# Graph convolution and GRU layer on one core: first group's setup without large GpSimd work, in another order

## The chip, the core and the metric

The kernel runs on one core of one Trainium2 chip. The metric is device time in microseconds. A program has five engines with a queue each: TensorE (PE), VectorE (DVE), ScalarE (ACT), GpSimd (POOL) and SyncE (SP), which here only issues DMAs.

## The reference, cut to what matters

Input `x` is 32 graphs x 256 nodes x 128 features in float32, `adj` is a 0/1 matrix of 256 x 256 for each graph.

```python
xc = transpose(x)                                  # features x nodes
h = relu(bn1(conv1(xc)))                           # 1x1 convolution
h = bn2(conv2(h))                                  # 17 taps along the nodes, padding 8
x_conv = transpose(relu(h + xc))
s = x @ w_se.T + b_se                              # 3 numbers a node
A = exp(-squared_distance(s)) * mask
x_nmp = A @ relu(x @ w_msg.T + b_msg)
gi, gh = concat(x_conv, x_nmp) @ w_ih.T + b_ih, x @ w_hh.T + b_hh
r, z = sigmoid(gi_r + gh_r), sigmoid(gi_z + gh_z)
out = layernorm(x + (1 - z) * tanh(gi_n + r * gh_n) + z * x)
```

## The kernel before, in words

The 32 graphs are taken in four groups of 8 (`NG`, `GB`), 2048 nodes each, in chunks of 512 columns. A float32 product is made of three matmuls in the rounded type fp32r: each operand is split into a high part, written by ACT (a copy into the fp32r tile), and a low part, the difference, written by DVE. `three` issues hi x hi, lo x hi and hi x lo (L324 is its matmul).

conv2 has 17 taps. The nodes of a graph lie in four phases (node number mod 4), and the kernel uses nine products (`PRODUCTS`, n = 0 to 8) in place of 16 phase pairs. Each has a "slot" of the activations (H3, D2, D3, E1, F0, F1, E3, F2, F3: a phase of conv1's output `H`, or differences of phases) and a weight set, 4 or 5 tap positions each: single taps of one phase f, or sums of taps. Product 0 uses the sum over all four phases (S0123), products 1 and 2 the sums 0+2 and 1+3, product 3 the sum 0+1, product 6 the sum 2+3, and products 4, 5, 7 and 8 the taps of phases 0, 1, 2 and 3. The results lie in `conv2_bank` in turn; ACT `shared` copies products 0, 3 and 6 out, DVE `product` adds the other six to these copies (`prod_used`), DVE `conv_sum` puts phases together and adds `x`, ACT `relu2` and DVE `conv_lo` make c_hi and c_lo.

Program order, for group 0 alone, is: conv1 on 4 chunks, "messages" for graphs 0 to 5 (relu(x W_msg), and the 3 numbers s), then `mix_stage(0, True)`: nine products of conv2, with other work put between them by `first_between`: messages 6 and 7, the transposes of the distance factors (`turn_rows`, read out by ACT `operands`), the distance matmuls (`distances`), and the gathers of the messages with A (`gather`). ACT `weights` is the exp, DVE `mask` the product with adj, ACT `sums_hi` and DVE `sums_lo` split the gathered sums into m_hi and m_lo. Then comes `gru_stage(0)`: per chunk, gate matmuls on x, m and c; in the same stage run conv1 and the messages of group 1. A loop runs `gru_stage(g)`, `mix_stage(g + 1, False)` for the other groups.

Setup that only group 0 pays: the tap sums (five tiles of 128 x 512), their hi and lo parts (`sum_hi`, `setup_sum_lo`), the hi and lo parts of the taps (`taps_hi` at L771, one ACT instruction of 2048 columns; `setup_taps_lo` at L947, four of 512), those of the gate weights (`gates_hi`, L775 and L777; `setup_gates_lo`, L926 and L927), and the slots of E and F over a whole group at once (`slot_high` L646, `slot_low` L989, `slot_f` L985). Before, POOL makes the tap sums 0+2 and 1+3 (L853), E low (L856, 1088 columns) and E high (L859, 1088 columns); DVE makes the sums 0+1, 2+3 (L922) and all four (L1309).

What sets the order is the program order of each engine's queue and semaphores: an instruction that waits holds all that stand behind it on its engine. SP's queue is the same: the issue of a DMA waits for a count, and later issues wait behind it. Buffers are shared in group 0: `x` holds four tap sums and later the real x, `ef` holds E and F, `adj[:, 1]` holds the rest of the gate weights, and `hn` and `z` hold small pieces.

```python
            def product(g, j, side, first):
                dve.wait_ge(s_ready, 3 * g + j + 1)
                dve.wait_ge(conv2_done, NP * g + n + 1)
```

Of the kernel before, what the change touches and what calls it, by code (L numbers as in the profile page):

```python
# [17 lines left out]
ALU = mybir.AluOpType  # L18
# [4 lines left out]
P = 128  # L23
# [53 lines left out]
def build(nc, xt_d, xn_d, adj_d, first_d, wsm_d, wcv_d, idn_d, bmsg_d, out_d):  # L77
    with ExitStack() as ctx:
# [53 lines left out]
        S_first = [x[:, CH:2 * CH], ef[:, SL:SL + CH], ef[:, 0:CH]]  # L132
# [4 lines left out]
        w_hhr = hn[:, 1, 0:P]  # L137
        w_rest = adj[:, 1, :, :, :].rearrange("p b m n -> p (b m n)")[:, 0:(NW - NF) * P]
# [4 lines left out]
        bmsg = z[0:2, 1, P:P + MW]  # L143

# [37 lines left out]
        bn1_ready, pool_sums_ready, idn_loaded = sem("bn1_ready"), sem("pool_sums_ready"), sem("idn_loaded")  # L182
# [3 lines left out]
        sum23_ready = sem("sum23_ready")  # L186
# [42 lines left out]
        def _(sp):  # L229
# [47 lines left out]
            sp.dma_start(w_rest, wsm_d[:, P:]).then_inc(gatesw_loaded, 16)  # L277
            sp.wait_ge(gatesw_ready, 1)
            load_adj(0, 1)
            load_adj_late(0, 2)  # L280
            sp.wait_ge(sum23_ready, 1)
            for k in range(NC):
                load_x(0, k)
            load_adj_late(0, 3)
            sp.wait_ge(cw_ready, NP - 1)
            for k in range(NC):
                load_xn(0, k)
            for s in range(2):
                sp.wait_ge(msg_done, 2 * s + 6)
                load_xs(1, s)  # L290
# [31 lines left out]
        def _(pe):  # L322
# [70 lines left out]
            def conv2(g, n, first):  # L393
# [9 lines left out]
                if first and n == 6:  # L403
                    pe.wait_ge(sum23_ready, 1)
                elif first:
                    pe.wait_ge(cw_ready, n + 1 if n < 6 else n)
# [17 lines left out]
            def first_between(n):  # L424
# [7 lines left out]
                elif n == 2:  # L432
                    distances(0, 0)
                    turn_rows(0, 1, True)
                elif n == 3:
# [151 lines left out]
        def _(act):  # L587
# [65 lines left out]
            def shared(g, j, first):  # L653
# [4 lines left out]
                if first:  # L658
                    act.wait_ge(*((cw_ready, 2), (slot_diff, 3), (slot_lo, 6))[j])
# [8 lines left out]
            def mix_stage(g, first):  # L668
                if first:
                    message(0, 6)  # L670
                    message(0, 7)
                    shared(g, 0, first)
                    slot_high(E1, E_all[:, 1], elow_ready, 1)
                    sum_hi(0)
                    operands(0, 0, True)
                    slot_high(F0, F_one, slot_diff, 1)
                    sum_hi(3)
                    gates_hi()
                    weights(g, 0)
# [5 lines left out]
                    slot_high(F1, F_one, slot_diff, 2)  # L685
                else:
# [8 lines left out]
                sums_hi(g, 0)  # L695
                shared(g, 1, first)
                weights(g, 4)
                if first:
                    slot_high(E3, E_all[:, 3], ehigh_ready, 1)
                    slot_high(F2, F_one, slot_diff, 3)  # L700
                sums_hi(g, 1)
                weights(g, 5)
                if first:
                    slot_high(F3, F_one, slot_diff, 4)
# [4 lines left out]
                weights(g, 7)  # L709
                sums_hi(g, 2)  # L710
# [72 lines left out]
            for k in (1, 2, 3):  # L783
                relu1(0, k, True)
            for k in (1, 2, 3):
                h3_hi(0, k)
            act.wait_ge(taps_loaded, 32)
            nc.scalar.activation(cw_hi[:, TAPS - 1:TAPS, :], last_tap, ACT.Copy).then_inc(cwhi_ready, 1)
            message(0, 0)
            act.wait_ge(tapsum_ready, 1)  # L790
            sum_hi(4)
            message(0, 1)
            d_hi(0, 0)
            message(0, 2)
# [18 lines left out]
        def _(pool):  # L813
# [41 lines left out]
            pool.wait_ge(h_ready, NC)  # L855
            nc.gpsimd.tensor_tensor(E_all[:, 0:2], H[:, 0:2, :], H[:, 2:4, :], ALU.subtract).then_inc(elow_ready, 1)  # L856
            pool.wait_ge(va_ready, NC)
            flat = H[:, :, :].rearrange("p a b -> p (a b)")
            nc.gpsimd.tensor_tensor(E_all[:, 2:4], H[:, 2:4, :],  # L859
                                    flat[:, 1:2 * SL + 1].rearrange("p (a b) -> p a b", a=2),  # L860
                                    ALU.subtract).then_inc(ehigh_ready, 1)
# [13 lines left out]
        def _(dve):  # L875
# [504 lines left out]
```

## Time and profile before

| what | us |
|---|---|
| median of 3 runs | 320.26 |
| the 3 runs | 319.72, 320.26, 322.0 |
| the profiled execution | 320.76 |
| its span, first to last instruction | 318.6 |
| TensorE busy in the span | 300.3 (94%) |
| VectorE busy | 251.5 (79%) |
| ScalarE busy | 155.9 (49%) |
| GpSimd busy | 31.1 (10%) |

The profiled execution is 2.16 us longer than its span; this part lies around the program. Times of rows count from the span's start. Mean granted TensorE clock: 0.982 of full speed.

### The profile page before, as it was taken

The page shows a single profiled execution, that of the slowest core. Times are in us where ns is not written, and L with a number is a line of the kernel's source. Part 1 is how long each engine was busy: PE and PEld are TensorE (multiplying, and loading weights), DVE is VectorE, ACT ScalarE, POOL GpSimd, SP SyncE. Part 2 cuts the span into 40 slices and gives each one's busy share as a digit, 9 for nine tenths or more (in the row PEclk, how much of TensorE's full clock was granted, in tenths as well). Part 3 has the DMA queues.
Part 4 walks back from the last instruction along what each step waited for, and adds up shares of the span by engine and source line. Part 5 has one row for each costly group of instructions (what it writes and reads, how often), then busy time and mean ns, then how long its engine had stood idle before and what let it go on. Part 6 is the DMA issues. An engine that isn't in the chain of part 4 may idle for free.

```text
span 318.6 us, 4624 instructions
## 1 busy us (share of the span) xinstructions
PE 300.3 (94%) x1422; PEld 240.6 (76%) x1422; DVE 251.5 (79%) x666; ACT 155.9 (49%) x326; POOL 31.1 (10%) x53
## 2 busy tenths in 40 slices
PE   8669989899999999999999999999999999999990
PEld 6457767778888778888888778888888778888860
DVE  3995869867977996967987996966987996963794
ACT  3753834338775622237775622237776613324345
POOL 3631000000000051000000041000000032000113
PEclk9959999999999999999999999999999999999997
DMA  7500161171210321171210231181210031150002
GB/s 224 214 1 2 65 224 41 66 265 64 69 34 32 103 97 68 69 263 37 80 47 21 88 122 66 66 263 35 66 51 14 32 132 66 44 154 0 0 35 99
DMA packets 12257, 27.23 MB, mean 85 GB/s; under 512 B 1363, under 2 KB 2133, under 8 KB 12117
## 3 DMA queue, kind: packets, MB, share of 16 engines
q1 hardware_dynamic: 12244, 27.08, 25.1%
q8 instruction: 6, 0.10, 0.1%
q14 instruction: 7, 0.05, 0.1%
HBM read 22.88 MB, written 4.19 MB: 85 GB/s over the span
## 4 chain that ended last, share of the span: by engine, by line
PE 81%; DVE 11%; ACT 2%; issue 2%; DMA 2%; POOL 0%; POOLq 0%; SPq 0%; ACTq 0%; DVEq 0%
PE bank L324 78%; DMA xr<-xt_dram 2%; PE bank L516 2%; PE bank L358 1%; DVE V_lo L969 1%; DVE H L1062 1%; DVE first L1096 1%; DVE V_lo L989 1%; DVE hn L1309 1%; DVE xr L1280 0%; DVE xr L1285 0%; ACT hn L745 0%; DVE x_lo L953 0%; DVE first L1102 0%; DVE H L1077 0%
## 5 line engine op out<-in xcount | busy, mean ns | idle before, releaser
L324 PE MATMUL bank<-V_hi,cw_hi 128*128 128x512 f32 x160 | 70.5, 440 | 2.8 <-ACT EF L661 1.4
L324 PE MATMUL bank<-V_lo,cw_hi 128*128 128x512 f32 x160 | 64.9, 406 | 0.0
L324 PE MATMUL bank<-V_hi,cw_lo 128*128 128x512 f32 x160 | 64.6, 404 | 0.0
L324 PE MATMUL bank<-x_hi,w_hl 128*128 128x512 f32 x128 | 47.3, 410 | 1.1 <-DVE x_lo L953 1.1
L324 PEld LDWEIGHTS bank<-V_hi,cw_hi 128*128 128x128 f32 x160 | 30.6, 191 | 11.0 <-issue 2.5
L324 PEld LDWEIGHTS bank<-V_hi,cw_lo 128*128 128x128 f32 x160 | 30.4, 190 | 8.4
L324 PEld LDWEIGHTS bank<-V_lo,cw_hi 128*128 128x128 f32 x160 | 30.5, 190 | 7.1
L324 PE MATMUL bank<-m_hi,w_hl 128*128 128x512 f32 x96 | 35.3, 400 | 0.6 <-DVE m_lo L1047 0.6
L324 PE MATMUL bank<-c_hi,w_hl 128*128 128x512 f32 x96 | 34.9, 396 | 0.0
L631 ACT ACTIVATE m_hi<-bank 128x512 fp32r<-128x512 f32 x16 | 9.6, 599 | 42.4 <-PE bank L324 42.4
L818 POOL TENSOR_TENSOR rstd<-first,pconst 128x4 f32<-128x4 f32 x16 | 3.5, 220 | 269.4 <-DVE first L1102 269.4
L324 PEld LDWEIGHTS bank<-x_hi,w_hl 128*128 128x128 f32 x128 | 24.1, 188 | 7.2 <-DVE x_lo L953 1.5
L1265 DVE SCALAR_TENSOR_TENSOR hn<-xr,hn 128x512 f32<-128x512 f32 x15 | 10.4, 692 | 20.5 <-ACT hn L733 20.5
L324 PE MATMUL bank<-x_lo,w_hl 128*128 128x512 f32 x64 | 25.2, 393 | 0.0
L732 ACT ACTIVATE xr<-bank,vec 128x512 f32<-128x512 f32 x16 | 11.0, 690 | 24.0 <-PE bank L324 24.0
L324 PEld LDWEIGHTS bank<-m_hi,w_hl 128*128 128x128 f32 x96 | 18.0, 188 | 5.1 <-DVE m_lo L1047 1.0
L324 PEld LDWEIGHTS bank<-c_hi,w_hl 128*128 128x128 f32 x96 | 18.0, 188 | 4.4
L324 PE MATMUL bank<-first,xr 128*128 128x132 f32 x128 | 20.0, 285 | 0.0
L666 ACT ACTIVATE c_hi<-H 128x512 fp32r<-128x512 f32 x16 | 10.2, 639 | 19.1 <-DVE H L1077 15.5
L1062 DVE SCALAR_TENSOR_TENSOR H<-bank,vec,EF 128x512 f32<-128x512 f32 x16 | 11.9, 746 | 9.1 <-PE bank L324 9.1
L324 PE MATMUL bank<-m_lo,w_hl 128*128 128x512 f32 x48 | 19.0, 396 | 0.0
L324 PE MATMUL bank<-c_lo,w_hl 128*128 128x512 f32 x48 | 19.0, 395 | 0.0
(135 smaller groups left out, 599.0 us busy)
## 6 DMA issues: line engine op xcount, KB each, us to landing
adj<-adj_dram SPq DMA_DIRECT2D x16, 512.0 KB, 4.4
x<-xt_dram SPq DMA_DIRECT2D x16, 256.0 KB, 3.1
xn<-xn_dram SPq DMA_DIRECT2D x16, 256.0 KB, 4.5
out_dram<-xn SPq DMA_DIRECT2D x15, 256.0 KB, 2.1
xr<-xt_dram SPq DMA_DIRECT2D x13, 256.0 KB, 3.5
xn<-wcv_dram SPq DMA_DIRECT2D x1, 1024.0 KB, 7.3
xr<-xt_dram SPq DMA_DIRECT2D x1, 768.0 KB, 6.0
adj<-wsm_dram SPq DMA_DIRECT2D x1, 512.0 KB, 7.8
```

Of the source, the lines that this page charges most:

```text
L324: return nc.tensor.matmul(out, lhs, rhs, start=start, stop=stop, skip_group_check=True)
L358: last = nc.tensor.transpose(out[:, i * N + mb * P:i * N + (mb + 1) * P], f32(U[:, i, mb]).rearrange("p b k -> p (b k)"), idn[:, :])
L516: turned = nc.tensor.transpose(turn_bank[k][:, j * P:(j + 1) * P], r[:, k % 2, j * P:(j + 1) * P], idn[:, :])
L631: nc.scalar.activation(chunk(m_hi, pair), nmp_bank[pair % 2][:, :], ACT.Copy).then_inc(mhi_ready, 1)
L666: nc.scalar.activation(phase(c_hi, c), inner(c), ACT.Relu).then_inc(chi_ready, 1)
L732: nc.scalar.activation(r[:, k % 2, :], r_bank[:, :], ACT.Tanh, bias=v(BR), scale=0.5).then_inc(r_ready, 1)
L818: nc.gpsimd.tensor_tensor(dst, src, eps.broadcast_to(shape), ALU.add).then_inc(eps_added, 1)
L969: TT(part(V_lo, H3, k), part(H, 3, k), f32(part(V_hi, H3, k)), ALU.subtract).then_inc(h3_ready, 1)
L989: TT(V_lo[:, slot, :], src, f32(V_hi[:, slot, :]), ALU.subtract).then_inc(slot_lo, 1)
L1062: STT(dst, grid(src), v(NSC2 if side else SC2), grid(shr), ALU.mult, ALU.add).then_inc(prod_used, 1)
L1096: last = nc.vector.bn_stats(stats[:, NB * k + j, :], node_rows(k)[:, j, :])
L1265: STT(hk, rk, 1.0, hk, ALU.add, ALU.mult).then_inc(gated_ready, 1)
```

## The change

POOL keeps only its small vectors. The tap sums 0+2 and 1+3, E low and E high go to DVE. The sum of all taps gets its hi and lo first, and the last tap follows. The taps are split phase by phase, each phase hi (`tap_hi`, 512 columns of stride) then lo, each counted in `cw_ready`. The first block of gate weights (`w_hhr`) moves to `z`, its split stays early; the rest of the gate weights (`w_rest`, 512 KB) is loaded into `ef` after the last F slot is made, and split at the end of the stage. `adj(0, 1)` is loaded at the start. `S_first` of products 3 and 6 moves to `xr`. PE's second `turn_rows` moves from product 2 to product 3. ACT's `operands(0, 0)` moves ahead of the split of E1. Waits change with that: x is loaded into `x` after the seventh weight set, xs for group 1 after `prod_used` 4 and 6.

```diff
-        S_first = [x[:, CH:2 * CH], ef[:, SL:SL + CH], ef[:, 0:CH]]
+        S_first = [x[:, CH:2 * CH], xr[:, 0], xr[:, 1]]
-        w_hhr = hn[:, 1, 0:P]
-        w_rest = adj[:, 1, :, :, :].rearrange("p b m n -> p (b m n)")[:, 0:(NW - NF) * P]
+        w_rest = ef[:, 0:(NW - NF) * P]
+        w_hhr = z[:, 1, CH - P:CH]
...
 SP:
             load_adj(0, 0)
-            sp.dma_start(w_rest, wsm_d[:, P:]).then_inc(gatesw_loaded, 16)
-            sp.wait_ge(gatesw_ready, 1)
             load_adj(0, 1)
             load_adj_late(0, 2)
-            sp.wait_ge(sum23_ready, 1)
+            sp.wait_ge(cw_ready, 7)
             for k in range(NC):
                 load_x(0, k)
+            sp.wait_ge(slot_diff, 4)
+            sp.dma_start(w_rest, wsm_d[:, P:]).then_inc(gatesw_loaded, 16)
             load_adj_late(0, 3)
-            sp.wait_ge(cw_ready, NP - 1)
+            sp.wait_ge(cw_ready, NP)
...
-                sp.wait_ge(msg_done, 2 * s + 6)
+                sp.wait_ge(prod_used, 4 + 2 * s)
                 load_xs(1, s)
...
 ACT mix_stage, first:
                     shared(g, 0, first)
+                    operands(0, 0, True)
                     slot_high(E1, E_all[:, 1], elow_ready, 1)
                     sum_hi(0)
-                    operands(0, 0, True)
                     slot_high(F0, F_one, slot_diff, 1)
-                    sum_hi(3)
-                    gates_hi()
+                    tap_hi(0)
                     weights(g, 0)
                     weights(g, 1)
-                    operands(g, 1, True)
-                    taps_hi()
+                    tap_hi(1)
+                    act.wait_ge(hhr_ready, 1)
                     weights(g, 2)
                     weights(g, 3)
+                    shared(g, 1, first)
+                    operands(g, 1, True)
                     slot_high(F1, F_one, slot_diff, 2)
+                    sum_hi(3)
...
                 weights(g, 7)
+                if first:
+                    gates_hi()
                 sums_hi(g, 2)
...
 POOL:
-            for i, a, b in ((1, 0, 2), (2, 1, 3)):
-                nc.gpsimd.tensor_tensor(tapsum[i], t[:, :, a, :], t[:, :, b, :], ALU.add).then_inc(pool_sums_ready, 1)
-            nc.gpsimd.tensor_tensor(E_all[:, 0:2], H[:, 0:2, :], H[:, 2:4, :], ALU.subtract).then_inc(elow_ready, 1)
-            nc.gpsimd.tensor_tensor(E_all[:, 2:4], H[:, 2:4, :],
...
 DVE:
+            def slots_e_low():
+                TT(E_all[:, 0:2], H[:, 0:2, :], H[:, 2:4, :], ALU.subtract).then_inc(elow_ready, 1)
...
                     product(g, 0, 0, first)
                     rows(g, 1, first)
+                    product(g, 0, 1, first)
                     slot_low(F0, F_one, 2)
+                    setup_tap_lo(0, 6).then_inc(cw_ready, 1)
+                    setup_hhr_lo()
+                    mask(g, 0)
+                    slots_e_high()
+                    mask(g, 1)
                     slot_f(1, 2)
-                    setup_gates_lo()
-                    product(g, 0, 1, first)
...
                 mask(g, 7)
+                if first:
+                    setup_gates_lo()
                 conv_sum(g, 2, first)
...
             TT(tapsum[4], tapsum[0], tapsum[3], ALU.add).then_inc(tapsum_ready, 1)
+            setup_sum(1, 0, 2).then_inc(tapsum_ready, 1)
+            setup_sum_lo(4, 1)
+            setup_last_tap_lo(2).then_inc(cw_ready, 1)
             for k in (1, 2, 3):
                 h3_lo(0, k)
-            setup_last_tap_lo(1)
...
+            setup_sum(2, 1, 3).then_inc(tapsum_ready, 1)
             for k in (2, 3):
                 d_lo(0, k)
             rows(0, 0, True)
             setup_sum_lo(2, 4).then_inc(cw_ready, 1)
+            dve.wait_ge(va_ready, NC)
+            slots_e_low()
```

The line numbers of the changed kernel differ. DVE's setup before, from the low part of H3's first quarter (V_lo is a slot's low part, x and hn hold tap sums, cw_lo is a low weight set, EF the D slots):

```order
L969 TENSOR_TENSOR V_lo<-H,V_hi 128x136 [waits h3hi_ready]
L922 TENSOR_TENSOR x<-xn 128x512 [waits taps_loaded]
L922 TENSOR_TENSOR x<-xn 128x512
L1309 TENSOR_TENSOR hn<-x 128x512 [waits setup_step]
L969 TENSOR_TENSOR V_lo<-H,V_hi 128x136 [waits h3hi_ready] x3
L939 TENSOR_TENSOR cw_lo<-z,cw_hi 128x128 [waits cwhi_ready]
L964 TENSOR_TENSOR EF<-H 128x136 [waits h_ready]
```

And the same place of the changed kernel:

```order
L964 TENSOR_TENSOR V_lo<-H,V_hi 128x136 [waits h3hi_ready]
L914 TENSOR_TENSOR x<-xn 128x512 [waits taps_loaded]
L914 TENSOR_TENSOR x<-xn 128x512
L1312 TENSOR_TENSOR hn<-x 128x512 [waits setup_step]
L914 TENSOR_TENSOR x<-xn 128x512
L930 TENSOR_TENSOR cw_lo<-hn,cw_hi 128x512 [waits cwhi_ready]
L934 TENSOR_TENSOR cw_lo<-z,cw_hi 128x128 [waits cwhi_ready]
L964 TENSOR_TENSOR V_lo<-H,V_hi 128x136 [waits h3hi_ready] x3
```

The sum 0+2 and the low part of the sum of all taps have moved in between the sums and the three low parts of H3. The second place is ACT at the start of the mix stage, before (msg and S: the copies of message 7; LR: `operands`; z and xr: `weights`):

```order
L611 ACTIVATE msg<-bank 128x256 [waits msg_done]
L612 ACTIVATE S<-bank 128x2x4
L661 ACTIVATE x<-bank,vec 128x512 [waits cw_ready,conv2_done]
L646 ACTIVATE V_hi<-EF 128x544 [waits elow_ready]
L768 ACTIVATE cw_hi<-x 128x512
L620 ACTIVATE LR<-bank 128x512 [waits lr_done]
L646 ACTIVATE V_hi<-EF 128x544 [waits slot_diff]
L768 ACTIVATE cw_hi<-x 128x512
L775 ACTIVATE w_hl<-hn 128x128 [waits hhr_loaded]
L777 ACTIVATE w_hl<-adj 128x1024 [waits gatesw_loaded]
L627 ACTIVATE z<-bank 128x512 [waits dist_done]
```

ACT there in the changed kernel:

```order
L608 ACTIVATE msg<-bank 128x256 [waits msg_done]
L609 ACTIVATE S<-bank 128x2x4
L658 ACTIVATE x<-bank,vec 128x512 [waits cw_ready,conv2_done]
L617 ACTIVATE LR<-bank 128x512 [waits lr_done]
L643 ACTIVATE V_hi<-EF 128x544 [waits elow_ready]
L773 ACTIVATE cw_hi<-x 128x512
L643 ACTIVATE V_hi<-EF 128x544 [waits slot_diff]
L777 ACTIVATE cw_hi<-xn 128x4x128
L624 ACTIVATE z<-bank 128x512 [waits dist_done]
```

LR has moved ahead of the first V_hi, which is the high part of E1; the gate weights are gone from here. The third place is ACT near the end of the stage, in the changed kernel, where before no row stands between the copy into xr and m_hi:

```order
L624 ACTIVATE xr<-bank 128x512 [waits nmp_done,dist_done]
L781 ACTIVATE w_hl<-EF 128x1024 [waits gatesw_loaded]
L628 ACTIVATE m_hi<-bank 128x512 [waits nmp_done]
```

The high part of the gate weights now stands, with its wait for a DMA, ahead of the third m_hi.

## Rows read from the trace of the kernel before

**Rows 1.** The page: busy time of the engines.

```profile
PE 300.3 (94%) x1422; PEld 240.6 (76%) x1422; DVE 251.5 (79%) x666; ACT 155.9 (49%) x326; POOL 31.1 (10%) x53
```

**Rows 2.** Windows: stretch, length, busy PE PEld DVE ACT POOL, PEclk, DMA, GB/s.

```profile
68.06:318.60 250.54, 242.61 (x1171) 195.85 (x1171) 199.31 (x556) 123.59 (x259) 19.54 (x32) 0.99 0.23 78
```

**Rows 3.** Chain that ended last: start us, us, what.

```profile
67.40 0.61 DVE m_lo L1047
...
68.06 13.29 PE bank L324 x61
```

**Rows 4.** Timeline of POOL: start us, us, engine, line, operation, tiles.

```profile
10.44 4.00 POOL L853 TENSOR_TENSOR x<-xn 128x512 f32<-128x512 f32 x2 [4.80 <-DMA z<-wcv_dram]
14.40 2.94 POOL L856 TENSOR_TENSOR EF<-H 128x1088 f32<-128x1088 f32 x1
22.68 2.12 POOL L859 TENSOR_TENSOR EF<-H 128x1088 f32<-128x1088 f32 x1 [5.34 <-DVE V_lo L974]
```

**Rows 5.** Timeline of DVE.

```profile
10.63 1.27 DVE L912 SCALAR_TENSOR_TENSOR bmsg_r<-bmsg_r,first,z 2x132 fp32r<-2x132 f32 x1
11.83 0.28 DVE L969 TENSOR_TENSOR V_lo<-H,V_hi 128x136 fp32r<-128x136 f32 x1
12.04 1.27 DVE L922 TENSOR_TENSOR x<-xn 128x512 f32<-128x512 f32 x2
13.35 1.65 DVE L1309 TENSOR_TENSOR hn<-x 128x512 f32<-128x512 f32 x1
14.91 3.00 DVE L969 TENSOR_TENSOR V_lo<-H,V_hi 128x136 fp32r<-128x136 f32 x3
22.83 2.04 DVE L1025 TENSOR_TENSOR U<-S,U 128x48 fp32r<-128x48 f32 x1
29.41 0.73 DVE L989 TENSOR_TENSOR V_lo<-EF,V_hi 128x544 fp32r<-128x544 f32 x1 [3.02 <-ACT V_hi L646]
33.23 0.21 DVE L1025 TENSOR_TENSOR U<-S,U 128x48 fp32r<-128x48 f32 x1
35.96 1.22 DVE L927 TENSOR_TENSOR w_hl<-adj,w_hl 128x1024 fp32r<-128x1024 f32 x1
```

**Rows 6.** Timeline of PE: message 4, conv2 products 0 and 1, first turn.

```profile
19.39 0.59 PE L324 MATMUL bank<-bmsg_r,ones_r 128*128 128x264 f32 x1 [2.50 <-ACT S L612]
...
21.61 0.78 PE L324 MATMUL bank<-V_hi,cw_hi 128*128 128x512 f32 x1
...
28.31 0.47 PE L324 MATMUL bank<-V_hi,cw_hi 128*128 128x512 f32 x1 [0.63 <-ACT S L612]
...
31.98 0.60 PE L358 MATMUL bank<-idn,U 128*128 128x128 f32 x4
```

**Rows 7.** Windows where the granted clock falls and comes back.

```profile
17.20:17.40 0.20, 0.00 (x0) 0.00 (x0) 0.20 (x1) 0.00 (x0) 0.14 (x1) 0.63 0.00 0
24.00:24.20 0.20, 0.20 (x2) 0.18 (x1) 0.20 (x1) 0.00 (x0) 0.20 (x1) 0.80 0.00 0
```

**Rows 8.** Timeline of ACT.

```profile
28.71 0.66 ACT L646 ACTIVATE V_hi<-EF 128x544 fp32r<-128x544 f32 x1
...
32.61 0.60 ACT L620 ACTIVATE LR<-bank 128x512 fp32r<-128x512 f32 x1 [2.71 <-PE bank L358]
...
34.37 1.05 ACT L777 ACTIVATE w_hl<-adj 128x1024 fp32r<-128x1024 f32 x1
```

**Rows 9.** Windows, the stretch from the low part of E1 to m_lo's end.

```profile
29.41:68.00 38.59, 35.92 (x167) 27.60 (x165) 31.52 (x58) 17.81 (x30) 0.00 (x0) 1.00 0.34 111
```

**Rows 10.** Waits of DVE, 29 to 69 us: total, times, longest.

```profile
DVE V_lo L989 <- ACT V_hi L646: 3.9, 2, 3.0
DVE m_lo L1047 <- ACT m_hi L631: 3.4, 2, 2.4
```

**Rows 11.** DMA issues up to 80 us: KB each, median us to landing.

```profile
x<-xt_dram SPq DMA_DIRECT2D x5, 256.0 KB, 5.7
...
adj<-wsm_dram SPq DMA_DIRECT2D x1, 512.0 KB, 7.8
```

More of the change, by code:

```diff
@@ L402, in conv2 @@
                     pe.wait_ge(vb_ready, 4 * g)
[L403 to L406, printed above, removed]
+                if first:
+                    pe.wait_ge(cw_ready, n + 1)
                 if n == 0 and not first:
@@ L433, in first_between @@
                     distances(0, 0)
+                elif n == 3:
                     turn_rows(0, 1, True)
-                elif n == 3:
                     gather(0, 0, True)
@@ L657, in shared @@
                     act.wait_ge(prod_used, 6 * g + 2)
-                if first:
-                    act.wait_ge(*((cw_ready, 2), (slot_diff, 3), (slot_lo, 6))[j])
+                if first and j == 0:
+                    act.wait_ge(cw_ready, 2)
                 src, dst = conv2_bank[(3 * j) % 2][:, :], (S_first if first else S_later)[j]
@@ L694, in mix_stage @@
                     weights(g, 3)
[L695 to L704, printed above, removed]
+                    sums_hi(g, 0)
+                    shared(g, 1, first)
+                    weights(g, 4)
+                    sums_hi(g, 1)
+                    weights(g, 5)
                 relu2(g, 0)
@@ L768, in sum_hi, with tap_hi @@
                 nc.scalar.activation(sums[:, s], tapsum[s], ACT.Copy).then_inc(cwhi_ready, 1)
-            def taps_hi():
-                nc.scalar.activation(cw_hi[:, 0:TAPS - 1, :], taps[:, :, :], ACT.Copy).then_inc(cwhi_ready, 1)
+            def tap_hi(f):
+                dst, src = (t[:, 0:TAPS - 1, :].rearrange("p (g k) o -> p g k o", k=4)[:, :, f] for t in (cw_hi, taps))
+                nc.scalar.activation(dst, src, ACT.Copy).then_inc(cwhi_ready, 1)
             def gates_hi():
-                act.wait_ge(hhr_loaded, 16)
-                nc.scalar.activation(w_hi[:, 1, :], w_hhr, ACT.Copy)
                 act.wait_ge(gatesw_loaded, 16)
@@ L975, in d_lo, with slots_e_high @@
                    ALU.subtract).then_inc(va_ready, 1)
+            def slots_e_low():
+                TT(E_all[:, 0:2], H[:, 0:2, :], H[:, 2:4, :], ALU.subtract).then_inc(elow_ready, 1)
+            def slots_e_high():
+                flat = H[:, :, :].rearrange("p a b -> p (a b)")
+                TT(E_all[:, 2:4], H[:, 2:4, :], flat[:, 1:2 * SL + 1].rearrange("p (a b) -> p a b", a=2),
+                   ALU.subtract).then_inc(ehigh_ready, 1)
             def slot_f(c, used):
@@ L1056, in product @@
                     dve.wait_ge(vb_ready, 4 * g)
-                if j == 0 and side == 1 and first:
-                    dve.wait_ge(gatesw_ready, 1)
                 P1 = P1_first if first else P1_later
@@ L1211, in mix_stage @@
                     norm_stats(prev, 3)
-                stats_done(3)
-                sums_lo(g, 0)
-                norm(norm_mean, 2)
-                norm(norm_mean, 3)
-                norm(normalise, prev, 0)
-                norm(normalise, prev, 1)
-                if first:
-                    slot_low(E3, E_all[:, 3], 4)
-                    slot_low(F2, F_one, 5)
-                    slot_f(3, 5)
+                    stats_done(3)
+                    sums_lo(g, 0)
+                    norm_mean(2)
+                    norm_mean(3)
+                    normalise(prev, 0)
+                    normalise(prev, 1)
                 product(g, 1, 0, first)
@@ L1237, in mix_stage @@
                 norm(normalise, prev, 3)
-                if first:
-                    setup_taps_lo(3, 7).then_inc(cw_ready, 1)
                 sums_lo(g, 2)
@@ L1243, in mix_stage @@
                 mask(g, 7)
+                if first:
+                    setup_gates_lo()
                 conv_sum(g, 2, first)
```

65 lines of the change are left out of this document (35 added, 30 removed).

## The prediction

> **What bounds the kernel now.** I read the busy times first, then windows, then the chain of waits, then the timelines of the first 30 us. TensorE is busy 94% of the span [rows 1]. From 68.06 us, where group 0's first gate matmuls on m begin, it is busy 242.61 of 250.54 us, and the chain there is TensorE alone for 13.29 us [rows 2, 3]. The change leaves the loop as it is, so I take what stands behind 68.06 as fixed: a gain or loss in time before that point is carried to the end unchanged. What ends last at 68.06 is DVE: m_lo (L1047) ends at 68.00, and the matmul behind it starts at once [rows 3]. So the question is when DVE writes the fourth m_lo.
>
> DVE's way there has two halves. From 10.6 to 26 us it shares the time with GpSimd's large operations, which run from 10.44 to 17.34 and from 22.68 to 24.80 [rows 4]. Just there DVE's instructions are long: the sum of all taps takes 1.65 us where two sums of the same shape take 1.27 together, three low parts of H3 take 3.00 where one takes 0.28, a small L1025 takes 2.04 where the same line takes 0.21 later, and L912 takes 1.27 [rows 5]. Each sits at the side of a GpSimd instruction. Over the port by these rows: 1.0 + 2.2 + 1.8 + 1.0, together 6.0 us of DVE. From 29.41, where the low part of E1 begins, to 68.00 DVE is busy 31.52 us of 38.59, so it waits 7.1 [rows 9]: 3.4 for m_hi, 0.9 for the high part of a slot (the 3.0 of the same row lie just ahead of 29.41) and the rest in smaller waits [rows 10].
>
> The Trainium skill, "SBUF — State Buffer", section "Who interferes with whom", says that VectorE and GpSimd share a port pair that one instruction holds exclusively, and only against certain VectorE forms, those with two SBUF inputs among them. The rows agree with the lock; by it nothing of the 6.0 us would stay, by a mere slowing of both some would. My sum takes all of it back either way, since no GpSimd instruction of that size is left.
>
> **The change part by part.**
>
> *Setup, to the first conv2 matmul.* DVE starts H3's first low part at 10.85 in place of 11.83 (L912 at the 0.2 of its neighbours). Then go two sums (1.2, by the 1.27 for two), the sum of all at 0.65, the added sum 0+2 at 0.6, the low part of the full sum at 0.6, the last tap at 0.2, and three H3 parts at 0.2: end at 15.3, against 17.91 before, though 1.4 us of work that stood later is now done. The D differences follow, so ACT's copies of messages 2 and 3 start at 16.6 and 16.9, and TensorE's message 4, which waited 2.50 us for such a copy until 19.39 [rows 6], starts at 17.1. Messages 4 and 5 take 1.0 us each at the low clock, 0.6 at the full one. conv2 starts at 18.6 instead of 21.61: -3.0.
>
> *Clock.* The granted clock is half (1.2 in place of 2.4 GHz) from 17.3 to 24.1 [rows 7]; the fall came 0.4 us into the gap of 2.50 that ends at 19.39 [rows 6], and before the rise TensorE had worked from 19.39 on. In the changed kernel ACT does the full sum and H3's high parts ahead of message 0, so TensorE's message 2 can start only at 15.0, 2.2 us behind the end of message 1; then comes a gap of 0.8, and work without a gap from 17.1. The fall will come, I think, and the rise at most as long behind the return of work as before, 4.7 us, which would be 21.8; since TensorE has also worked between the two gaps, I take 20.7. Product 0 then runs 2.05 us at 0.43 us a matmul and the rest at 0.24, 4.6 us in all as before (4.8), and product 1 starts at 25.1 against 28.31: -3.2. Ends for this term: never low gives product 1 at 23.8 (1.3 better), low until 24.1 gives 26.6 (1.5 worse).
>
> *E low* (1088 columns) on DVE: 1.3 us by the 1.22 us of 1024 columns [rows 5]. It ends at 22.9; DVE then waits for E1's high part anyway, so it costs nothing.
>
> *E1 behind the turn.* ACT now takes `operands(0, 0)`, which needs TensorE's turn behind product 1, ahead of E1's high part. Before, E1's high part ran at 28.71, three and a half us ahead of the turn [rows 6, 8]. Now: product 1 from 25.1, 3.67 us as before (28.31 to 31.98), turn 0.4, hop 0.2, operands 0.5, high part 0.7: E1's low part starts on DVE at 30.7, against 29.41 [rows 5]. This gives back 1.3 us of DVE's start. DVE idles some 7.8 us ahead of it.
>
> *From there to m_lo 4.* DVE's work is that of before, 31.5 us, plus E high at 1.3 (the two tap sums are done in setup; the gate weights' low part, 1.22, only changes its place). Its waits of 7.1 us go almost all: TensorE and ACT are now ahead of it, because product 2 starts at 29.2 instead of 32.3 while DVE starts later. What is left, instruction by instruction: 0.3 for F1's high part, 1.1 for m_hi 3 (on ACT it stands behind the gate weights' high part, 1.05 us [rows 8]), 0.8 for c_hi 3; say 2.2. Busy times count about 0.08 us of tail at each wait, so with fewer waits the sum 30.7 + 31.5 + 1.3 + 2.2 = 65.7 is an upper value, 64.9 the one reckoned by starts. I take 65.2 against 68.06: **-2.9 us**. TensorE on this way waits 0.6 for product 3, 1.1 for gather 6, 1.8 ahead of the m part; it is no longer what DVE waits for.
>
> *DMA.* x is issued when the seventh weight set is ready, at 43.2, and needed by `conv_sum(0)` at 48.0. Before, the chunks landed in 5.7 us with 1 MB of adj ahead of them [rows 11]; now one adj load is ahead by 3 us, and I take the last of four at 4.6 after the first issue: no wait, up to 1.1 us if it is 5.7 for the last. The rest of the gate weights is issued at 46.2 and needed by ACT at 55.5: 9.2 us against the 7.8 that the same load took [rows 11], hidden. xs for group 1 comes after xn at 55, earlier than before; its second half waits until product 6's sum at 63.6 and is needed 9 us later. The early load of adj(0, 1) takes the place of an equal load.
>
> The profiled execution is 320.76, which gives 317.9. It lies 0.5 above the median 320.26; from the median the same difference gives **317.4**, and runs are compared by medians.
>
> **The rivals.**
>
> *A, the clock hardly falls.* For it: work is denser from 15.0 on. Against: there is a gap of 2.2 us, and before it fell 0.4 us into one. Product 1 would start at 23.8, everything behind it moves with DVE's start: 1.3 more, 320.26 - 4.2 = 316.0. The Trainium skill, "TensorE: Matmul & The Clock Gate", in its table of practical rules, asks only for no gap above some 3 us; by it this is the outcome, 316.0. But in this trace the clock fell with no gap longer than 2.5 us [rows 6, 7], so I give it less than its page would.
>
> *B, x or ACT makes DVE wait in the mix stage.* x landing at 5.7 us costs 1.1; waits of the kind of rows 10 left to half (3 more than I take off) cost up to 1.5. 318.5 to 319.
>
> *C, the new order only moves the wait.* DVE starts its stretch 1.3 us later, and if the clock rises at 24.1 or later it starts 2.7 later: m_lo ends at 66.5 to 67.2: 318.8 to 319.6, hardly a change.
>
> *D, slower: the gate weights' DMA.* ACT waits for it in the queue ahead of m_hi 3, and c_hi 3, m_hi 4 and c_hi 4 are behind; DVE's m_lo 3 and TensorE's gates wait in turn. The price is one for one beyond 9.2 us of landing; it makes the kernel slower from 9.2 + 2.9 = 12.1 us on. Against it: the same load landed in 7.8 with 2 MB ahead of it. At 14 us: 322.2.
>
> **How the numbers follow.** Forecast 0.50, A 0.17, B 0.18, C 0.11, D 0.04. About 1% (3.2 us) is what a measurement of this kernel tells from no change; faster by over 1% is below 317.06. Of the forecast, whose own range is 316.6 to 318.2, not quite half lies there, 0.22, and with A it is 0.39; slower 0.03 from D; the rest, 0.58, is within 1%. The range 315.7 to 319.4 leaves out D, the best of A and the worst of C.
>
> **What would show it.** In the changed profile: no DVE instruction of 136 columns above 0.35 us ahead of 30 us; conv2's first matmul at 18 to 19; the clock low from some point ahead of 18 to about 21; DVE idle for 7 to 8 us ahead of E1's low part at about 30.7; then hardly a wait until m_lo 3; the fourth m_lo ends at 65 to 65.7, and TensorE's busy share behind it as before. It would be wrong if the stretch behind the m matmuls is not 250.5 us long any more, if DVE waits for x or for ACT in the middle, or if the clock falls again later.

## The result, and the profile after

| | us |
|---|---|
| kernel before, median of 7 runs | 320.94 (319.72 to 322.15) |
| changed kernel, median of 7 runs | 319.04 (316.68 to 319.45) |
| ratio, 95% interval | 0.9924, 0.9897 to 0.9951 |
| profiled execution before / after | 320.76 / 318.56 |
| its span before / after | 318.6 / 316.8 |

By the ratio the change gives 0.76%, some 2.4 us of the 320.94; the two medians lie 1.9 us apart. A gain of 2.9 had been forecast, and 317.4 for the time. The profiled executions differ by 2.2 us, their spans by 1.8.

First the page and two windows of the changed kernel: busy times; then the stretch from group 0's first matmul on m to the end (as in [rows 2]), and the one from E1's low part to the end of the fourth m_lo (as in [rows 9]).

```profile
PE 298.6 (94%) x1422; PEld 239.7 (76%) x1422; DVE 248.7 (79%) x670; ACT 156.3 (49%) x329; POOL 21.9 (7%) x49
```

```profile
66.24:316.80 250.56, 242.62 (x1171) 195.84 (x1171) 199.26 (x556) 123.51 (x259) 19.45 (x32) 0.99 0.23 79
30.51:66.18 35.67, 31.74 (x146) 24.02 (x145) 32.27 (x59) 17.44 (x32) 0.00 (x0) 1.00 0.35 112
```

Behind the m matmuls the two kernels are alike: 250.54 us before, 250.56 now, with the same busy times. All of the change lies ahead of 66.24, which was 68.06. GpSimd has 9.2 us less to do.

The timeline of DVE in the changed kernel (its lines differ: L1312 is the sum of all taps, L964 the low parts of H3, L1028 the small operation that was L1025, L992 a slot's low part, L1071 the first step of `conv_sum(0)`, L1050 m_lo, L974 and L978 E low and E high):

```profile
11.09 0.34 DVE L904 SCALAR_TENSOR_TENSOR bmsg_r<-bmsg_r,first,z 2x132 fp32r<-2x132 f32 x1
12.88 0.69 DVE L1312 TENSOR_TENSOR hn<-x 128x512 f32<-128x512 f32 x1
15.09 0.71 DVE L964 TENSOR_TENSOR V_lo<-H,V_hi 128x136 fp32r<-128x136 f32 x3
20.51 0.21 DVE L1028 TENSOR_TENSOR U<-S,U 128x48 fp32r<-128x48 f32 x1
22.17 1.28 DVE L974 TENSOR_TENSOR EF<-H 128x1088 f32<-128x1088 f32 x1
30.51 0.73 DVE L992 TENSOR_TENSOR V_lo<-EF,V_hi 128x544 fp32r<-128x544 f32 x1 [7.05 <-ACT V_hi L643]
37.11 1.29 DVE L978 TENSOR_TENSOR EF<-H 128x1088 f32<-128x1088 f32 x1
49.43 0.69 DVE L1071 TENSOR_TENSOR H<-hn,H 128x512 f32<-128x512 f32 x1 [1.54 <-DMA x<-xt_dram]
58.50 0.69 DVE L1050 TENSOR_TENSOR m_lo<-bank,m_hi 128x512 fp32r<-128x512 f32 x1 [0.82 <-ACT m_hi L628]
65.50 0.68 DVE L1050 TENSOR_TENSOR m_lo<-bank,m_hi 128x512 fp32r<-128x512 f32 x1
```

The four long instructions of [rows 5] are short: 1.65 has become 0.69, 3.00 is 0.71, 2.04 is 0.21, 1.27 is 0.34. E low and E high cost 1.28 and 1.29. DVE then stands idle for 7.05 us ahead of E1's low part, and it has a wait that the kernel before did not have: 1.54 us for the DMA of x.

TensorE in the same execution, messages 2 and 4, and conv2 products 0, 1, 3 and 7, gather 6 and the m part (DVE's L1063 is `product`, L1045 `mask`):

```profile
15.44 0.39 PE L323 MATMUL bank<-bmsg_r,ones_r 128*128 128x264 f32 x1 [2.15 <-ACT S L609]
17.50 0.59 PE L323 MATMUL bank<-bmsg_r,ones_r 128*128 128x264 f32 x1
19.41 0.48 PE L323 MATMUL bank<-V_hi,cw_hi 128*128 128x512 f32 x1
25.03 0.47 PE L323 MATMUL bank<-V_hi,cw_hi 128*128 128x512 f32 x1 [0.63 <-ACT S L609]
33.28 0.47 PE L323 MATMUL bank<-V_hi,cw_hi 128*128 128x512 f32 x1 [0.64 <-DVE hn L1063]
52.86 0.47 PE L323 MATMUL bank<-V_hi,cw_hi 128*128 128x512 f32 x1 [0.96 <-DVE H L1063]
57.74 1.13 PE L323 MATMUL bank<-z,msg 128*128 128x256 f32 x4 [0.90 <-DVE z L1045]
66.24 0.50 PE L323 MATMUL bank<-m_hi,w_hl 128*128 128x512 f32 x1 [1.48 <-DVE m_lo L1050]
```

Product 1 begins at 25.03 against 28.31 [rows 6]. From there to the m part TensorE waits four times for more than 0.5 us, each time for DVE. The granted clock falls and comes back here (windows, the last but two columns):

```profile
15.60:15.80 0.20, 0.20 (x2) 0.20 (x3) 0.20 (x2) 0.20 (x3) 0.00 (x0) 0.76 0.00 0
19.00:19.20 0.20, 0.20 (x3) 0.20 (x3) 0.20 (x1) 0.20 (x2) 0.00 (x0) 0.71 0.00 0
```

It is low for 3.4 us, half the 6.8 of [rows 7].

**One ruler for all kernels.** The second chunk of conv1 starts by when the x load has landed, at 9.2 to 10.0 us, and that differs between executions of one kernel. So I measure three stretches of one profiled execution of each kernel: *setup*, from there ("start" in the table) to product 1; *stage*, from product 1 to the first m matmul; and *rest*, to the end of the span, which is 250.45 to 250.60 in all fourteen. The column "clock low" covers the time up to 70 us.

| kernel | start | clock low | setup | stage | median us | ratio to before |
|---|---|---|---|---|---|---|
| before | 9.31 | 17.3-24.1 | 19.00 | 39.75 | 320.94 | 1 |
| changed | 9.78 | 15.7-19.1 | 15.25 | 41.21 | 319.04 | 0.9924 |
| after_again | 9.57 | 15.8-19.2 | 15.39 | 40.71 | 318.21 | 0.9900 |
| dummy_idle | 9.82 | never | 14.50 | 41.14 | 319.02 | 0.9926 |
| dummy_dense | 9.56 | 15.8-19.2, 60.0-63.5 | 15.38 | 43.66 | 320.83 | 0.9978 |
| e_on_pool | 9.57 | 15.2-25.4 | 19.32 | 39.66 | 320.55 | 0.9962 |
| x_early | 10.03 | 9.8-13.1 | 15.19 | 39.14 | 316.47 | 0.9838 |
| e1_first | 9.75 | 15.5-18.9 | 15.21 | 38.48 | 315.45 | 0.9822 |
| fill | 9.29 | never | 14.51 | 38.53 | 316.19 | 0.9849 |
| fill_tail | 9.66 | 17.4-20.8 | 16.09 | 37.62 | 315.32 | 0.9808 |
| fill_e1_tail | 9.84 | 17.7-21.2 | 16.09 | 37.57 | 315.54 | 0.9815 |
| keep_clock_after | 9.23 | never | 14.50 | 41.27 | 318.18 | 0.9911 |
| keep_clock_before | 9.53 | never | 17.13 | 39.75 | 319.29 | 0.9940 |
| fill_e1_tail_keep | 9.65 | never | 14.50 | 37.57 | 313.96 | 0.9778 |

In x_early the clock was low during conv1, and not in the gap behind message 1. The change won 3.75 us in setup and lost 1.46 in the stage; 0.47 went the other way with the start. Together 1.82, the difference of the spans. A stretch comes from a single execution: the stage of the changed kernel is 41.21 in the first profile and 40.71 in after_again.

### The profile page after: what moved, and what is told of

Read it like the earlier page. It is cut to its first block, busy times and chain, and to the rows that moved or that the text cites. A ratio compares the mean times of both kernels' runs of the same rounds, so it can differ in the third digit from the quotient of the medians.

```text
span 316.8 us, 4627 instructions
## 1 busy us (share of the span) xinstructions
PE 298.6 (94%) x1422; PEld 239.7 (76%) x1422; DVE 248.7 (79%) x670; ACT 156.3 (49%) x329; POOL 21.9 (7%) x49
## 3 DMA queue, kind: packets, MB, share of 16 engines
q1 hardware_dynamic: 12244, 27.08, 25.4%
## 4 chain that ended last, share of the span: by engine, by line
PE 76%; DVE 12%; DMA 4%; ACT 3%; issue 3%; SPq 1%; POOL 0%; POOLq 0%; ACTq 0%; DVEq 0%
PE bank L323 73%; DMA xr<-xt_dram 2%; PE bank L513 2%; DMA x<-xt_dram 2%; PE bank L357 1%; DVE first L1097 1%; DVE H L1063 1%; DVE V_lo L992 1%; DVE xr L1045 1%; DVE xr L1283 0%; DVE xr L1288 0%; ACT hn L750 0%; DVE x_lo L948 0%; DVE H L1071 0%; DVE first L1103 0%
## 5 line engine op out<-in xcount | busy, mean ns | idle before, releaser
L323 PEld LDWEIGHTS bank<-x_hi,w_hl 128*128 128x128 f32 x128 | 24.1, 188 | 8.4 <-DVE x_lo L948 2.2
L1268 DVE SCALAR_TENSOR_TENSOR hn<-xr,hn 128x512 f32<-128x512 f32 x15 | 10.4, 691 | 21.2 <-ACT hn L738 21.2
L323 PEld LDWEIGHTS bank<-first,xr 128*128 128x128 f32 x128 | 18.6, 203 | 0.2
```

What stands on the lines that cost most here:

```text
L323: return nc.tensor.matmul(out, lhs, rhs, start=start, stop=stop, skip_group_check=True)
L1268: STT(hk, rk, 1.0, hk, ALU.add, ALU.mult).then_inc(gated_ready, 1)
```

## The experiments

### Does a large GpSimd operation block DVE?

**e_on_pool.** E low and E high go back to GpSimd, the rest stays as changed:

```diff
 POOL:
+            pool.wait_ge(h_ready, NC)
+            nc.gpsimd.tensor_tensor(E_all[:, 0:2], H[:, 0:2, :], H[:, 2:4, :], ALU.subtract).then_inc(elow_ready, 1)
+            pool.wait_ge(va_ready, NC)
+            nc.gpsimd.tensor_tensor(E_all[:, 2:4], H[:, 2:4, :],
...
 DVE:
-            slots_e_low()
-                    slots_e_high()
```

> The changed kernel with E low and E high back on GpSimd, all else as changed. Theory 1 (DVE is blocked for as long as a large GpSimd operation runs): DVE's setup stretches by the 2.9 us of E low and some 2 of E high, conv2's first matmul moves from 19.4 to 21.5 or later, E1's low part from 30.5 to 32.5-33.5, the later stretch is 1.3 shorter without E high, the m matmuls of group 0 begin at 67-68.5 against 66.24, and the time is 1 to 2 us above the changed kernel's 319.0. Rival (the two engines share a port only by slowing, and the gain came from the order): the m matmuls begin at about 65, 1.3 us earlier.

Measured: 320.55 us, ratio 0.9962 (0.9941 to 0.9984), the m matmuls at 68.55. GpSimd and DVE of this kernel side by side (timelines; L922 is the sum 0+2, L1036 the small one of 0.21):

```profile
12.84 2.88 POOL L856 TENSOR_TENSOR EF<-H 128x1088 f32<-128x1088 f32 x1 [7.21 <-ACT H L602]
22.25 2.11 POOL L859 TENSOR_TENSOR EF<-H 128x1088 f32<-128x1088 f32 x1 [6.54 <-DVE V_lo L977]
```

```profile
13.28 2.98 DVE L922 TENSOR_TENSOR x<-xn 128x512 f32<-128x512 f32 x1
22.40 2.03 DVE L1036 TENSOR_TENSOR U<-S,U 128x48 fp32r<-128x48 f32 x1
```

The first of the two DVE instructions starts 0.44 us after the GpSimd one and ends 0.5 us behind it; the second ends 0.07 behind its neighbour. They are 2.3 and 1.8 us too long, however little they have to do (48 columns). Setup grows by 4.1 us, from 15.25 to 19.32, and the two GpSimd operations account for it together with the clock, which is low for some 10 us in this execution; this run does not separate their shares. E1's low part follows product 1 (28.89) and starts at 34.37, later than the 33.5 I had allowed. The stage is 1.55 shorter: E high's 1.3 is gone and the wait for x is 0.4 instead of 1.54, of which other waits take part back. The rival, which had the m matmuls at about 65, is refuted. The time is 1.5 us above the changed kernel's 319.04, as expected, though the intervals of the two ratios overlap a little.

**dummy_idle and dummy_dense.** Two GpSimd additions that nothing needs, in DVE's wait or in its dense stretch:

```diff
+            pool.wait_ge(elow_ready, 1)      # dummy_idle
+            pool.wait_ge(prod_used, 4)       # dummy_dense
+            pool.wait_ge(x_ready, 2)
+            for i in range(2):
+                nc.gpsimd.tensor_tensor(chunk(m_lo, 2 + i), f32(chunk(x_lo, 0)), f32(chunk(x_lo, 1)),
+                                        ALU.add).then_inc(spare_done, 1)
...
+                    dve.wait_ge(spare_done, 2)      # ahead of the third m_lo
```

> The changed kernel plus two GpSimd additions of 128x512 into a tile that is rewritten later, released when E low is ready, so that they run beside DVE's wait ahead of E1's low part (23.5 to 30.5). Output unchanged. Both theories: no DVE instruction grows, the time stays within 0.3 us of the changed kernel. It is the control for dummy_dense.

> The same two additions, released by the fourth use of a product (about 52.7), where DVE works without a pause. Theory 1 (lock, and DVE's work sets the end of the stage): they take some 4 us, DVE instructions beside them stand for 2 us each, the m matmuls of group 0 begin 2.5 to 4 us later than 66.24 and the time rises by as much. Rival (mere slowing, or TensorE sets the end): under 1 us.

Measured: 319.02 us (ratio 0.9926, 0.9900 to 0.9953) beside the idle DVE, as the changed kernel; 320.83 (0.9978, 0.9958 to 0.9997) in the dense stretch. GpSimd in dummy_idle and in dummy_dense:

```profile
23.56 2.51 POOL L859 TENSOR_TENSOR m_lo<-x_lo 128x512 fp32r<-128x512 f32 x2 [17.79 <-DVE EF L981]
```

```profile
52.90 3.40 POOL L859 TENSOR_TENSOR m_lo<-x_lo 128x512 fp32r<-128x512 f32 x2 [47.21 <-DVE H L1070]
```

and DVE in dummy_dense, the low parts of F3 and of a tap phase:

```profile
53.34 1.82 DVE L999 TENSOR_TENSOR V_lo<-EF,V_hi 128x544 fp32r<-128x544 f32 x1
55.08 1.77 DVE L949 TENSOR_TENSOR cw_lo<-xn,cw_hi 128x512 fp32r<-128x512 f32 x1
```

Two neighbours grow by 1.1 us each, 2.2 together, and GpSimd itself takes 3.40 for what it does in 2.51 alone: each waits for the other. The stage grows by 2.5 us against the first profile of the changed kernel. I had asked for 2.5 to 4 at the m matmuls and as much in the time; the m matmuls come 2.36 later, and the medians of the two dummies lie 1.8 apart. So the sign and the place are right, and the size is that of what DVE loses (2.2, and 0.2 in a longer wait for x), less than the GpSimd time and a little less than I had asked for.

A side effect has to be ruled out: TensorE waits 3.10 us for DVE here, and the clock falls a second time, to half from 60.0 to 63.5:

```profile
60.04 2.01 PE L324 MATMUL bank<-z,msg 128*128 128x256 f32 x4 [3.10 <-DVE z L1052]
67.86 0.68 DVE L1057 TENSOR_TENSOR m_lo<-bank,m_hi 128x512 fp32r<-128x512 f32 x1
68.60 0.50 PE L324 MATMUL bank<-m_hi,w_hl 128*128 128x512 f32 x1
```

From the start of that `mask` (59.30 here, 57.00 in the changed kernel) to the start of the fourth m_lo are 8.56 us here and 8.50 there. So DVE paced the end all the same, and the low clock used up the 1.48 us that TensorE otherwise waits ahead of the m part.

### Where did the stage lose 1.5 us?

**x_early.** The split of tap sum 2+3 goes into the idle time, and with it x can be loaded earlier:

```diff
 SP:
-            load_adj_late(0, 2)
-            sp.wait_ge(cw_ready, 7)
+            sp.wait_ge(cw_ready, 5)
+            sp.wait_ge(prod_used, 2)
             for k in range(NC):
                 load_x(0, k)
+            load_adj_late(0, 2)
 PE:
-                    pe.wait_ge(cw_ready, n + 1)
+                    pe.wait_ge(cw_ready, (1, 2, 3, 5, 6, 7, 7, 8, 9)[n])
 DVE, ahead of slots_e_low():
+            setup_sum_lo(3, 5).then_inc(cw_ready, 1)
```

> The changed kernel with the hi and lo of tap sum 2+3 in DVE's and ACT's idle time ahead of E1, and the x load released by the second use of a product, about 8 us earlier. Theory 1 (DVE's work and waits set the end, the wait for x counts in full): the 1.5 us wait ahead of conv_sum(0) is gone and 0.6 us of DVE work left the dense stretch, the m matmuls begin at 64.2 in place of 66.24, the time falls by 2 us. Rival (TensorE or ACT is just behind DVE): it falls by less than 1 us, and the waits of DVE for m_hi grow.

Measured: 316.47 us, ratio 0.9838 (0.9811 to 0.9864), the m matmuls at 64.36. The wait for x is gone and the one ahead of E1's low part is partly filled; those for m_hi and c_hi are as they were (waits of DVE, total, times, longest):

```profile
DVE V_lo L993 <- ACT V_hi L644: 5.7, 1, 5.7
DVE m_lo L1051 <- ACT m_hi L629: 0.8, 1, 0.8
DVE c_lo L1083 <- ACT c_hi L664: 0.7, 1, 0.7
```

The stage is 2.07 us shorter, the 1.54 and 0.6 of the expectation.

**e1_first.** Only the order on ACT:

```diff
                     shared(g, 0, first)
-                    operands(0, 0, True)
                     slot_high(E1, E_all[:, 1], elow_ready, 1)
                     sum_hi(0)
+                    operands(0, 0, True)
```

> The changed kernel with ACT's high part of E1 and of sum 0+1 put back ahead of operands(0, 0), nothing else. Theory 1 (DVE's start into the stage counts, the changed order costs 1.3 us or more): E1's low part starts at 26.1 in place of 30.5, part of this is lost in waits for TensorE's products 1 and 2, the m matmuls begin at 64.4 against 66.24 and the time falls by 1.8. Rival (TensorE paces the products, the early start turns into waits for it): under 0.6.

Measured: 315.45 us, ratio 0.9822 (0.9781 to 0.9862), the m matmuls at 63.44. DVE in this kernel:

```profile
26.06 0.72 DVE L992 TENSOR_TENSOR V_lo<-EF,V_hi 128x544 fp32r<-128x544 f32 x1 [2.65 <-ACT V_hi L643]
```

E1's low part starts 4.4 us earlier and 2.7 of it are gained in the stage, 0.9 more than reckoned (2.2 against the stage of after_again, from the same set of runs). DVE's waits list 2.1 us for TensorE's products in return and no wait for x. Against the changed kernel in the same set of runs (318.21) this is 2.8 us from three lines. So the new place of `operands(0, 0)` is the dearest part of the change. Its price includes the wait for x, which the earlier start takes away too (1.54 us in the first profile, 1.06 in after_again), so it does not add up with x_early's gain.

**fill and fill_tail.** fill is x_early with the low parts of sum 0+1 and of `w_hhr`, and E high, behind `slots_e_low()` in the idle time. fill_tail adds:

```diff
 ACT:
+                if first:
+                    gates_hi()
                 shared(g, 2, first)
...
                 weights(g, 7)
-                if first:
-                    gates_hi()
 DVE:
                 mask(g, 6)
                norm(normalise, prev, 3)
+                if first:
+                    setup_gates_lo()
                 sums_lo(g, 2)
...
                 mask(g, 7)
-                if first:
-                    setup_gates_lo()
```

> x_early, with the low parts of sum 0+1 and of the first gate block and E high also moved into DVE's idle time ahead of E1 (2.0 us more out of the dense stretch). If DVE's work alone sets the end: the m matmuls begin at 62.4. If TensorE takes over, as reckoned from its rows: 63.7, only 0.6 better than x_early's 64.36, with new waits of DVE for high parts (F1, F2).

> fill, with the split of the rest of the gate weights taken out of the end: ACT's high part ahead of shared(2), DVE's low part in its wait ahead of the third m_lo. Theory 1: behind the last gather only DVE's tail counts, it is 1.1 us shorter: the m matmuls begin at 62.6, TensorE's wait ahead of them falls from 1.5 to below 1, the time is 3.5 to 4 us below the changed kernel. Rival (the tail waits for something else, such as the gathers): no gain over fill.

Measured: fill 316.19 (0.9849, 0.9814 to 0.9883), fill_tail 315.32 (0.9808, 0.9765 to 0.9851). By the stage: 39.14 (x_early), 38.53, 37.62. Moving 2.0 us of DVE work brought 0.6, as reckoned for TensorE taking over; the tail brought 0.9, and TensorE's wait ahead of the m part is 0.59:

```profile
25.75 0.47 PE L324 MATMUL bank<-V_hi,cw_hi 128*128 128x512 f32 x1 [0.63 <-ACT S L610]
...
63.37 0.50 PE L324 MATMUL bank<-m_hi,w_hl 128*128 128x512 f32 x1 [0.59 <-DVE m_lo L1051]
```

The medians of fill and x_early are 0.3 us apart with intervals that overlap; only the profiles order them. I compare stages, because the m matmuls themselves also move with the clock in setup: in fill they begin at 62.33, close to the 62.4 of "DVE's work alone", but product 1 began 1.4 us earlier there than in x_early, half of it by the start and half in setup, where the clock never fell; in fill_tail they begin at 63.37, not 62.6. fill_tail is 2.9 us below the changed kernel of the same set (318.21), not 3.5 to 4.

**after_again.** The changed kernel in the same set of runs:

> The changed kernel itself, as measure for the other three on the same chip: the m matmuls begin within 1 us of 66.24, by when the clock falls and rises.

Measured: 318.21, ratio 0.9900 (0.9865 to 0.9935). Its wait for x was 1.06 us where the first profile shows 1.54, and its stage 0.50 shorter.

**fill_e1_tail.** fill_tail with E1's and F0's high parts ahead of `operands(0, 0)` on ACT, and F0's low part ahead of the first `product` on DVE:

> fill_tail with the high parts of E1 and F0 ahead of operands(0, 0) too. In fill_tail TensorE waits only 0.6 us between product 1 and the m matmuls, so if TensorE bounds there now, the stretch stays at 37.6 us (fill_tail) within 0.3. If DVE still paces it: 1 to 2 us shorter.

Measured: 315.54 (0.9815, 0.9774 to 0.9856), stage 37.57 against 37.62: no gain. TensorE is busy 36.91 us of the 37.57, so it bounds the stage (window from product 1 to the m matmuls):

```profile
25.93:63.50 37.57, 36.91 (x170) 28.60 (x171) 30.04 (x56) 18.49 (x33) 0.00 (x0) 1.00 0.32 107
```

DVE now starts 4.2 us earlier and waits later instead. What was worth 2.7 us alone is worth nothing measurable here.

### What is the clock's share?

**keep_clock_after and keep_clock_before.** Matmuls of no use in TensorE's gap, seven behind message 1 of the changed kernel, nine behind message 3 of the one before:

```diff
+            def keep(n):
+                for _ in range(n):
+                    mm(bank[6][:, :], ones_r[:, :], ones_r[:, :].rearrange("p (o d) -> p o d", o=1).broadcast_to([P, 4, P]),
+                       start=True, stop=True)
...
                 messages(0, b, True)
+                if b == 3:      # 1 in the changed kernel
+                    keep(9)     # 7
```

> The changed kernel with seven matmuls of no use (constants into bank 6, which product 0 overwrites) behind message 1, in TensorE's gap of 2.15 us. If the clock keeps 2.4 GHz, product 1 begins at 24.3 in place of 25.0 (as in the one run where the clock did not fall), the m matmuls at about 65.5 and the time falls by 0.7; the single times scatter less. Rival (the gap does not decide): the clock falls at 15 to 17 all the same, no change.

> The kernel before with nine such matmuls behind message 3, in the gap of 2.50 us ahead of 19.39. Theory 2 (a good part of the change's gain is the clock: 3.3 us low in place of 6.8): product 0 is done in 3.7 us instead of 4.8, messages 4 and 5 in 1.2 instead of 2.2, product 1 begins at 25.9 in place of 28.31, and 1.5 to 2.4 us of this stay, so the kernel before with this alone would be as fast as the changed one. Theory 1 (DVE, stretched by GpSimd, paces the setup and the stage): at most 0.8 us stay at the m matmuls, though product 1 begins earlier.

Measured: 318.18 (0.9911, 0.9878 to 0.9945) and 319.29 (0.9940, 0.9922 to 0.9958). The clock did not fall in either profile. keep_clock_before:

```profile
15.93 2.32 PE L324 MATMUL bank<-ones_r 128*128 128x512 f32 x9
19.80 0.39 PE L324 MATMUL bank<-bmsg_r,ones_r 128*128 128x264 f32 x1 [1.55 <-ACT S L619]
...
66.41 0.50 PE L324 MATMUL bank<-m_hi,w_hl 128*128 128x512 f32 x1 [0.56 <-DVE m_lo L1054]
```

Its ten times lie within 319.16 to 320.10, those of the kernel before within 320.27 to 322.35. Setup is 1.87 us shorter, the stage is 39.75 to the hundredth as before, so all of it stays, and my "at most 0.8" is refuted (product 1 begins at 26.66, not at 25.9). In the changed kernel the same cure takes setup from 15.25 to 14.50, 0.75; its median against 319.04 and 318.21 is not told apart, and its four times do not scatter less (1.15 us, against 1.10 in after_again). Filling the gap does not exclude a fall either: one of the four, at 318.31 us, has a mean granted clock of 0.985, the other three 0.993.

So the change's 3.75 us in setup divide, by one profile of each kernel: 1.87 - 0.75 = 1.12 from a shorter time at the low clock, 2.63 (17.13 to 14.50) from DVE's work. With the clock kept in both, the change is worth 318.18 against 319.29, 1.1 us by medians and 1.4 by the spans, of which 0.3 is the start; the stretches give 1.1 (2.63 less the 1.52 by which the stage grew). That is about half of the 2.3 us that setup and stage gave together without the filling (3.75 less 1.46); the other half is the clock.

**fill_e1_tail_keep.** All of it together:

> The same with the seven matmuls of keep_clock_after. Setup and stage as before, product 1 about 0.7 to 1.4 us earlier than with the fall of the clock: 314.3 to 314.8, the least time of all.

Measured: 313.96 us, just below the 314.3 to 314.8 expected, the four times within 313.88 to 314.26, ratio 0.9778 (0.9745 to 0.9811). It beats both kernels: 2.2% below the one before, 1.3 to 1.6% below the changed one. Setup 14.50, stage 37.57, rest 250.48.

## Why the prediction was right, point by point

The sign, the place of the gain and the whole range (315.7 to 319.4) were right. The size was too large: the median 319.04 lies outside the forecast's own 316.6 to 318.2, where rivals B (318.5 to 319) and C (318.8 to 319.6) stood, and of the 2.9 us forecast at the m matmuls 1.8 came.

- **What bounds the kernel.** Right: DVE's fourth m_lo released the m matmuls in thirteen of the fourteen profiles (in dummy_dense TensorE came free at the same moment), and the rest kept its 250.5 us in each.
- **Setup.** Right in sum: product 1 was put at 25.1 and began at 25.03. That is partly luck, because two parts in it were off and cancelled: conv2 began at 19.41, not 18.6, since the messages 2 to 5 all ran at the low clock and the start was 0.5 later, and product 0 then ran wholly at the full clock. DVE's part was well reckoned: from the first low part of H3 to the end of the last it took 4.43 us, where the forecast had 10.85 to 15.3; the terms that it lists add up to less, some 4.1.
- **Clock.** The fall was forecast, the rise put at 20.7 and seen at 19.1 here, at 20.8 and 21.2 in fill_tail and fill_e1_tail; in dummy_idle and fill there was no fall though TensorE's gap of 2.15 to 2.17 us was the same. What rival A describes did not happen in the changed kernel's profile, but in those two it did, and the one run of the changed kernel with a mean clock of 0.993 (the other six have 0.982 to 0.989) took 316.68 us, near rival A's 316.0. The filled gap prices it at 0.75 us in setup, where the forecast had 1.3. The forecast counted the 3.2 us at product 1 in the sum, but did not see the shorter low clock as a cause of its own: 1.1 of the 3.75 us is the clock. The Trainium skill, "TensorE: Matmul & The Clock Gate", in its table of practical rules, would have no fall here; dummy_idle and fill agree with it, the changed kernel's profile, with no gap above 2.2 us in setup, does not.
- **The port.** Right: the 6.0 us read from four long rows vanished, and e_on_pool and dummy_dense bring such rows back. Not every neighbour pays: before, two sums of 128x512 took 1.27 us together beside GpSimd's additions, as without them, and the two GpSimd additions took 4.00 there [rows 4, 5] against 2.51 for two of the same size alone in dummy_idle. That suggests that GpSimd waited there; its inputs have other strides, so it is not shown. The Trainium skill, "SBUF — State Buffer", section "Who interferes with whom", calls it an exclusive lock; these traces agree, with two neighbours of 2.2 us in all beside 3.40 us of GpSimd, and with 48 columns that take 2.03.
- **E1 behind the turn.** Place and size right: 30.7 forecast (its terms add up to 30.6), 30.51 seen, against 29.41 before.
- **From there to m_lo 4.** 65.2 was forecast, 66.24 seen. The forecast's upper sum was 30.7 + 31.5 + 1.3 of work + 2.2 of waits = 65.7; measured are 30.51 + 32.27 + 3.40, so the work was 0.5 less and the waits were 1.2 more. The term that failed is the landing of x: "I take the last of four at 4.6 after the first issue: no wait, up to 1.1 us". The issue came at 42.95, the last landed 4.94 us after its own issue at 44.27, 6.3 after the first, and DVE waited 1.54. The term left out that SP's last issue comes 1.3 us behind the first; the remaining 0.4 is the landing itself. Rival B had it at 1.1 and was a part of the outcome, and "if DVE waits for x" was one of the prediction's own signs of being wrong. x_early removed it and got it back in full. The other waits stood where they were put: 0.82 for m_hi 3 (1.1), 0.71 for c_hi 3 (0.8), and none of weight for F1's high part.
- **Rival D** did not occur: the gate weights landed in 5.0 us, where the reckoning allowed 9.2.
- **The signs.** Seen: short instructions of 136 columns, 7.05 us of idle time ahead of E1's low part, no second fall of the clock, the rest unchanged. Missed: conv2 at 18 to 19 (19.41), the clock low to about 21 (19.1), the fourth m_lo ending at 65 to 65.7 (66.18).

What the forecast did not ask is what the new order costs: it took the 1.3 us later start as given. e1_first shows 2.7 us to be had there; its earlier x load also spares the wait for x.

## What to carry to other kernels

Before work is taken off one engine to free another, look for instructions that are far longer than the same shape elsewhere: here four of them held most of what GpSimd cost DVE, and the profile lists them as busy time, not as waits. When an instruction is put in a strict queue ahead of another that waits for less, price what stands behind it. And of several cures in one stage each counts in full only until the next engine bounds: 2.7 us alone, nothing behind two others.

## What was not expected of the hardware

- Kernels with the same program up to there show the clock falling or not: in setup TensorE's waits were alike (2.15 to 2.17 us ahead of message 2), and it was low for 3.4 us in the changed kernel, not at all in dummy_idle and fill, and from 17.4 or 17.7 in two others. fill_e1_tail's four times spread over 1.6 us, and with the gap filled four spread over 0.4; in the changed kernel the filling narrowed nothing. In e_on_pool, where a second gap of 1.59 us follows the first, it was low for some 10 us.
- In the window from 0 to 7 us the trace of before gives the full clock, yet 14 matmuls of 512 columns that start there take 6.10 us, 0.44 each, while the same matmuls at 15.93 us of keep_clock_before take 2.32 for nine, 0.26 each. So ahead of the first change of the clock in a trace I do not read the granted clock from it, and take no argument from that stretch; why they are slow there was not tried. The row of before:

```profile
1.31 6.10 PE L324 MATMUL bank<-ones_r 128*128 128x512 f32 x14 [1.31 <-DVE ones_r L896]
```

- A GpSimd addition slows under DVE as well (1.26 us alone, 1.70 beside it), so both engines pay for the overlap.
